# The first inverse transform in pieces of 128 rows by 64 columns, with its first product made between the pieces

## The reference, cut to what matters

```python
x_ft = jnp.fft.rfft2(xt, s=(M, N)) / scale_fwd
a = x_ft[:, :, :nm, :nm]
blk1, blk2 = _complex_matmul_2d(a, fw1), _complex_matmul_2d(a, fw2)
out_ft = out_ft.at[:, :, :nm, :nm].set(blk1)
out_ft = out_ft.at[:, :, N - nm:, :nm].set(blk2)
out = jnp.fft.irfft2(out_ft, s=(N, M)) / scale_bwd
res = out @ W + b
return jax.nn.relu(res + out)
```

## Time and profile before

| what | us |
|---|---|
| median of 3 runs (lowest, highest) | 14682.73 (14680.42, 14685.68) |
| the profiled execution, its own time | 14687.5 |
| its span in the profile | 14685.3 |
| TensorE busy | 10796.8 |
| VectorE busy | 8873.9 |
| ScalarE busy | 6706.6 |
| GpSimd busy | 5138.0 |

### The profile page before, as it was taken

One profiled execution on the slowest core, in us unless ns is written; L12 is line 12 of the kernel. 1 busy time (PEld: TensorE's weight loads), 2 busy tenths in 40 slices (PEclk: granted clock), 3 DMA queues, 4 the chain that ended last, 5 costly groups with the idle time before them and its releaser, 6 DMA issues. The chain is left out here.

```text
span 14685.3 us, 297339 instructions
## 1 busy us (share of the span) xinstructions
PE 10796.8 (74%) x113226; PEld 7857.0 (54%) x113226; DVE 8873.9 (60%) x20267; ACT 6706.6 (46%) x10775; POOL 5138.0 (35%) x3844
## 2 busy tenths in 40 slices
PE   8655665999999999787787879986774677454432
PEld 3243222777777777666666668852322333344432
DVE  3213444777777777788888843322544545599992
ACT  5311222777777777566666632245233444222220
POOL 0002443656555655433333345520000689200001
PEclk9878887999999999999999989998787888555555
DMA  6686775111111111111111159997899666300008
GB/s 261 186 183 187 241 234 188 40 40 43 40 43 40 43 40 41 47 46 70 47 54 62 47 209 363 363 327 257 315 377 384 234 200 221 86 25 23 18 10 324
DMA packets 1298491, 2188.40 MB, mean 149 GB/s; under 512 B 116749, under 2 KB 951069, under 8 KB 1231781
## 3 DMA queue, kind: packets, MB, share of 16 engines
q1 hardware_dynamic: 878084, 1649.47, 33.9%
q10 hardware_dynamic: 398624, 463.54, 8.9%
q0 software_dynamic: 20608, 58.22, 1.4%
HBM read 1371.45 MB, written 799.58 MB: 148 GB/s over the span
## 5 line engine op out<-in xcount | busy, mean ns | idle before, releaser
L781 POOL TENSOR_TENSOR la_s<-la_s,la_mx 128x512 f32<-128x512 f32 x2048 | 2093.2, 1043 | 1458.0 <-DVE la_mx L740 1457.6
L820 ACT ACTIVATE la_et<-la_pt 128x512 f32<-128x512 f32 x2048 | 1120.2, 598 | 723.4 <-PE la_pt L652 723.4
L652 PE MATMUL la_pt<-la_idn,la_s 128*128 128x128 f32 x8192 | 1174.4, 289 | 214.8 <-POOL la_s L781 214.3
L740 DVE TENSOR_REDUCE la_mx<-la_s 128x16 f32<-128x1024 f32 x1024 | 1243.0, 1214 | 17.7
L732 DVE TENSOR_TENSOR la_s<-la_ps,la_post 128x2048 f32<-128x2048 f32 x512 | 1167.5, 2280 | 25.1 <-PE la_ps L638 25.1
L652 PEld LDWEIGHTS la_pt<-la_idn,la_s 128*128 128x128 f32 x8192 | 921.6, 146 | 328.1 <-issue 224.2
L2252 ACT ACTIVATE cs_sm<-cs_sm,cs_gq,cs_tt 8x1 f32<-8x1 f32 x1024 | 395.0, 386 | 1187.6 <-DVE cs_sm L2336 1187.6
L2135 PE MATMUL cs_tb<-cs_tt,cs_sel 8*128 8x16 f32 x2048 | 448.2, 370 | 652.6 <-DVE cs_tt L2334 652.6
L1439 PE MATMUL pj_pp<-pj_pw,pj_at 128*128 128x256 f32 x4096 | 927.5, 380 | 0.0
L956 PE MATMUL gm_xp<-gm_fws,gm_y 128*128 128x258 f32 x2048 | 561.6, 421 | 421.7 <-ACT gm_ri L1040 421.7
L1439 PEld LDWEIGHTS pj_pp<-pj_pw,pj_at 128*128 128x128 f32 x4096 | 759.3, 190 | 92.9
(11 more groups left out here) (327 smaller groups left out, 27151.3 us busy)
## 6 DMA issues: line engine op xcount, KB each, us to landing
f_xt<-in_x SPq DMA_DIRECT2D x128, 1024.0 KB, 7.9
i_xr<-in_x SPq DMA_DIRECT2D x64, 2048.0 KB, 9.0
x<-pj_o SPq DMA_DIRECT2D x64, 2048.0 KB, 10.2
f_xt<-x SPq DMA_DIRECT2D x128, 1024.0 KB, 13.7
i_xr<-x SPq DMA_DIRECT2D x64, 2048.0 KB, 14.5
x<-i_xo ACTq DMA_DIRECT2D x64, 2048.0 KB, 14.6
sp_xt<-x SPq DMA_DIRECT2D x144, 512.0 KB, 4.6
out<-sp_xt SPq DMA_DIRECT2D x144, 512.0 KB, 2.9
```

The costliest lines, as they stand in the source:

```text
L652: last = nc.tensor.transpose(t_bank(S, i)[:, h, :], s[:, S % RS, i, h, :], idn[:, :])
L740: nc.vector.reduce_max(mx[:, S % RS, ts, :].rearrange("p t h -> p (t h)"), s[:, S % RS, ts].rearrange("p t h (d i) -> p (t h d) i", d=2), ...
L781: nc.gpsimd.tensor_tensor(sv, sv, mb, ALU.subtract).then_inc(s_sub, 1)
L820: nc.scalar.activation(et[:, k % RT].rearrange("p h n -> p (h n)"), t_bank(S, i)[:, :, :].rearrange("p h n -> p (h n)"), ACT.Exp).then_inc ...
```

## The change

Each image is cut in 8 pieces again, but of 128 rows and 64 columns (r = k % 2, columns 64 * (k // 2) on), so a piece has the same 2 MB. A load is now 128 runs of 16 KB. A store run is 8 windows of 32 channels, 1 KB, and a piece has two stores of 1 MB; SP asks for them, behind the load of the piece two later. The first product is cut in units of eight channels and 128 columns, 16 units an image (NU = 8 for each half of the columns), eight matmuls each. A unit fills `zp`, two PSUM banks of its own, and waits until the unit before it is emptied. The eight units of the right half are made during pieces 0 to 2 of the image, after the matmuls 1, 3 and 5 of a piece; those of the left half of the next image during pieces 5 to 7. VectorE empties the even ones, behind the additions of one more matmul, ScalarE the odd ones. The squares of a piece are summed in the piece that follows, after its matmul 6. The totals of an image come after piece 0 of the next, the statistics after pieces 1 and 2. The modes of the next image are asked for behind the load of piece 4 and the stores of piece 2. All loops are written out.

```diff
-    WC = 32
-    NP = W // WC
+    WC = 64
+    NP = 2 * W // WC
...
+    ALL = B * NP
+    SPOTS = (1, 3, 5)
...
+        zp = m.ps("zp", [P, 2, 512])
...
+        def unit_at(q, i):
+            b, k = q // NP, q % NP
+            if i not in SPOTS or k in (3, 4):
+                return None
+            n = (k if k < 3 else k - 5) * len(SPOTS) + SPOTS.index(i)
+            if n >= NU or (k > 4 and b + 1 == B):
+                return None
+            return b * 2 * NU + (NU if k < 3 else 2 * NU) + n
...
+                def load(q):
+                    b, k = q // NP, q % NP
+                    r, w0 = k % 2, k // 2 * WC
+                    if q >= 2:
+                        sp.wait_ge(s_fused, (q - 1) * NB)
+                    sp.dma_start(xr[:, q % 2, :], res[b, r * P:(r + 1) * P, w0:w0 + WC, :].rearrange("p w c -> p (w c)"))\
+                        .then_inc(s_x[q % 2], 16)
+                def store(q):
...
+                    sp.wait_ge(s_fused, (q + 1) * NB)
+                    for s, out in enumerate((out_l, out_g)):
+                        sp.dma_start(out[b, r * P:(r + 1) * P, :, n0:n0 + NW, :].rearrange("p u n c -> p u (n c)"),
+                                     xo[:, q % 2, s * CH:(s + 1) * CH].rearrange("p (u m) -> p u m", u=WIN)).then_inc(s_store[q % 2], 16)
+                for q in range(ALL):
+                    load(q)
+                    if q >= 2:
+                        store(q - 2)
+                    if q % NP == 4 and q // NP + 1 < B:
+                        sp.wait_ge(s_u, (q // NP + 1) * 2 * NU)
+                        modes(q // NP + 1)
...
+                def unit(u):
+                    pe.wait_ge(s_zb, 2 * (u // (2 * NU)) + 2)
+                    if u:
+                        pe.wait_ge(s_v[(u - 1) % 2], (u - 1) // 2 + 1)
+                    n = u % NU
+                    for k in range(4):
+                        for h in range(2):
+                            rows = slice(h * kr, (h + 1) * kr)
+                            last = nc.tensor.matmul(zp[:, h, k * P:(k + 1) * P], zv[rows, :, 8 * n + 2 * k + h],
+                                                    km[rows, columns(u)], start=True, stop=True)
+                    last.then_inc(s_u, 1)
...
+                for q in range(ALL):
...
+                    for i in range(NB):
+                        n = q * NB + i
+                        if n >= 4:
+                            pe.wait_ge(s_fused, n - 3)
+                        nc.tensor.matmul(fp[:, n % 4, :], kxm[:, r * P:(r + 1) * P],
+                                         v[:, w0 + i * WIN:w0 + (i + 1) * WIN, :].rearrange("p w c -> p (w c)"),
+                                         start=True, stop=True).then_inc(s_f, 1)
+                        u = unit_at(q, i)
+                        if u is not None:
+                            unit(u)
+                        if i == 6 and q:
+                            if k == 1 and b:
+                                group_sums(b - 1)
+                            squares(q - 1)
...
+                for q in range(ALL):
+                    b, k, j = q // NP, q % NP, q % 2
+                    dve.wait_ge(s_x[j], 16 * (q // 2 + 1))
+                    if q >= 2:
+                        dve.wait_ge(s_store[j], 32 * (q // 2))
+                        dve.wait_ge(s_acc, q - 1)
+                        dve.wait_ge(s_sq, q - 1)
+                    for i in range(NB):
+                        dve.wait_ge(s_f, q * NB + i + 1)
...
+                        last.then_inc(s_fused, 1)
+                        u = unit_at(q, i - 1)
+                        if u is not None and u % 2 == 0:
+                            turn(u)
+                    if k == 0 and b:
+                        totals(b - 1)
...
-                        for s, out in enumerate((out_l, out_g)):
-                            for r in range(2):
-                                act.dma_start(out[bass.ds(b, 1), r * P:(r + 1) * P, :, wc * NW:(wc + 1) * NW, :]
...
+                    act.wait_ge(s_fused, (q + 1) * NB)
+                    if q:
+                        act.wait_ge(s_sum, q)
+                    nc.scalar.activation(sq[:, :], xo[:, q % 2, :], ACT.Square).then_inc(s_sq, 1)
```

More of the change, by code:

```diff
@@ L2552, in _ @@
+                for q in range(ALL):
[5 more added lines that the diff above has]
+                        modes(q // NP + 1)
+                for q in range(ALL - 2, ALL):
+                    store(q)
+                for j in range(2):
+                    sp.wait_ge(s_store[j], 32 * (ALL // 2))
             @block.tensor
@@ L2619, in _ @@
+                squares(ALL - 1)
+                group_sums(B - 1)
             @block.vector
             def _(dve):
[L2621 to L2624 removed]
                 nc.vector.memset(ones[:, :], 1.0).then_inc(s_ones, 1)
@@ L2630, in _, with add_bias, turn, totals @@
                     row = brow[h * kr:h * kr + 1, :]
-                    last = nc.vector.tensor_scalar(row, row, bias_scale, None, ALU.mult)
-                last.then_inc(s_ones, 1)
-                dve.wait_ge(s_ones, 4)
+                    nc.vector.tensor_scalar(row, row, bias_scale, None, ALU.mult).then_inc(s_ones, 1)
+                dve.wait_ge(s_ones, 5)
+                def add_bias(b):
+                    dve.wait_ge(s_z, b * 32 + 32)
+                    for h in range(2):
+                        row = zx[h * kr:h * kr + 1, 0, 0, :]
+                        nc.vector.tensor_tensor(row, row, brow[h * kr:h * kr + 1, :], ALU.add).then_inc(s_zb, 1)
+                def turn(u):
+                    dve.wait_ge(s_u, u + 1)
+                    nc.vector.tensor_copy(*evict(u)).then_inc(s_v[0], 1)
+                def totals(b):
+                    dve.wait_ge(s_acc, b * NP + NP)
+                    if b:
+                        dve.wait_ge(s_tp, b)
+                    for h in range(2):
+                        cs = slice(h * HALF, (h + 1) * HALF)
+                        last = nc.vector.reduce_sum(tot[:, 0, cs], acc[:, h * CH:(h + 1) * CH].rearrange("p (n c) -> p c n", c=HALF),
+                                                    axis=AX.X)
+                    last.then_inc(s_accfree, 1)
+                    dve.wait_ge(s_sum, b * NP + NP)
+                    for h in range(2):
+                        rows, cs = slice(h * 64, (h + 1) * 64), slice(h * HALF, (h + 1) * HALF)
+                        last = nc.vector.reduce_sum(tot[rows, 1, cs], sums[rows, :].rearrange("p (n c) -> p c n", c=HALF), axis=AX.X)
+                    last.then_inc(s_tot, 1)
                 def finish(b):
@@ L2705, in _ @@
+                totals(B - 1)
+                finish(B - 1)
+                deviation(B - 1)
             @block.gpsimd
             def _(pool):
[L2707 to L2717 removed]
+                for q in range(ALL):
+                    b, k = q // NP, q % NP
+                    pool.wait_ge(s_fused, (q + 1) * NB)
+                    if k == 0:
+                        if b:
+                            pool.wait_ge(s_accfree, b)
+                        nc.gpsimd.tensor_copy(acc[:, :], xo[:, q % 2, :]).then_inc(s_acc, 1)
+                    else:
+                        pool.wait_ge(s_acc, q)
+                        nc.gpsimd.tensor_tensor(acc[:, :], acc[:, :], xo[:, q % 2, :], ALU.add).then_inc(s_acc, 1)
@@ L2752, in _ @@
-                for_images(act, body, finish)
-                for j in range(2):
-                    act.wait_ge(s_store[j], (B * (NP // 2) + 1) * 64)
-                act.wait_ge(s_sst, B * 16 + 16)
+                for u in range(1, NU, 2):
+                    turn(u)
+                for q in range(ALL):
+                    b, k = q // NP, q % NP
+                    for i in SPOTS:
+                        u = unit_at(q, i)
+                        if u is not None and u % 2:
+                            turn(u)
+                    if k == 2 and b:
+                        deviation(b - 1)
+                    if k == 3 and b:
+                        put_stats(b - 1)
+                    act.wait_ge(s_fused, (q + 1) * NB)
+                    if q:
+                        act.wait_ge(s_sum, q)
+                    nc.scalar.activation(sq[:, :], xo[:, q % 2, :], ACT.Square).then_inc(s_sq, 1)
```

227 lines of the change are left out of this document (64 added, 163 removed).

## The result

The changed kernel takes 14635.8 us (median of 7 runs, 14629.3 to 14643.7) against 14682.7: a ratio of 0.9967, with a 95% interval of 0.9956 to 0.9977. That is 47 us less (0.33%), where 249 were forecast, and above the range's end of 14600. The profiled execution took 14633.8, with a span of 14632.1.

The account below looks back on a forecast made before the run. Pieces were taken as DMA-bound, the first product as TensorE and evicting engines with DMA idle. Prologue 47.7, images 993 and ending 22.7 gave stage 1063, 249 less, so 14434; 8-in-10 range 14350 to 14600.

Parts of the forecast that it names:

- the working of an image, 128: One image in the stage: pieces 105, totals 7, modes 11, clock 5, against 161 before.
- I take 1.1: First product: one unit of 16 instructions lasts 1.1 us, range 0.9 to 1.5, upper end 2.2 if nothing ran side by side.
- TensorE's whole work for an image: 90: TensorE at full clock: second product, squares and 16 units total 90 us an image, under 12.1 a piece.
- VectorE: ... 72 and a few small ones: VectorE per image: additions, eight evictions and totals total 72 us; small operations not priced.
- my rivals: TensorE cold half the time (0.15, 14592); transfers no cheaper (0.14, 14530); better (0.06, 14290 to 14330); slower (0.05, 14865).
- So 1.5 of wait in each piece that has units: Single `zp`: TensorE waits 1.5 us per piece with units while VectorE empties an even unit behind its addition.
- I take 13: Loading an image's modes, 4.2 MB in the same queue, takes 13 us, between 11.5 and 15.1.
- 1 KB stores at 46.6 ns: Store transfers: 2048 runs of 1 KB at 46.6 ns cost 5.96 us a piece, against 7.05 with 512 bytes.
- That all stores move to SP's queue costs me nothing: Issuing all stores from SP adds no time; ScalarE's freed squares are already counted in the 12.1 a piece.
- The idle third: First product between images, 40.6 us with DMA engines 1% busy, which the change was to fill.
- The clock: TensorE's granted clock above 0.9 after dense work; 5 us an image added for 90 of work.
- DMA share below 0.75 and VectorE waits mostly for `fp`: Sign in the changed stage that the forecast was wrong on the waits.

Follow-up runs that it names:

- with the waits removed: Changed kernel with statistics in PSUM, VectorE emptying units before additions, modes laid out by halves in one 128-partition DMA, two buffers, asked earlier: 14375.1, ratio 0.9791.
- The order alone: Changed kernel with VectorE emptying an even unit before its next addition instead of behind it: 14579.6, ratio 0.9928.
- The transfers alone: Kernel before with 128-row by 64-column pieces, 16 KB loads, 1 KB stores still asked for by ScalarE, first product between images: 14648.4, ratio 0.9974.
- taking its freedom back: Changed kernel with stores asked for by ScalarE again, ahead of the square; loads and modes stay on SP: 14746.5, ratio 1.0043.
- three were joined: Changed kernel with statistics and bias scratch in PSUM, VectorE emptying units before additions, mode load in eight alternating DMAs: 14497.2, ratio 0.9874.

## Why the prediction was wrong

The forecast had the place and the direction right and missed four fifths of the size. What failed is the working of an image, 128, in three of its terms: a unit at 1.1, the small VectorE operations at nothing, and the mode load at 13. By piece, against its own working (13.8 with three units, 12.7 with two, 12.1 without, 7 for totals, 11 for modes, and 5 an image for the clock):

| pieces of the image | forecast | measured | what made the difference |
|---|---|---|---|
| 0 and 6 | 27.6 | 33.4 | six units, 0.92 more each |
| 7 | 12.7 | 16.1 | two units, and a second product partly at a lower granted clock (0.89 in the window) |
| 1, with the totals | 20.8 | 20.4 | none |
| 2 and 3, with the statistics | 24.8 | 41.0 | VectorE held by GpSimd |
| 4 | 12.1 | 8.9 | the load had long landed |
| 5, with the modes | 24.8 | 34.1 | the modes, and the load and stores behind them |
| clock | 5 | | in the rows above |
| sum | 128 | 153.9 | |

26 more an image, by 7.5, are 195 of the 200 that the stage missed.

- **"I take 1.1" for a unit: wrong.** It measured 2.02, near the upper end of 2.2. The Trainium skill's rule beside it ("TensorE: Matmul & The Clock Gate", LDWEIGHTS, estimate 1.7) was nearer. My range took units up to 1.5 only, though I had written 2.2 as the bound. Worth 57 by the run with half of the loads. "TensorE's whole work for an image: 90" fell with it: TensorE was busy 116.4 of the 153.9, and with the waits removed still 89% of 119.7, some 107.
- **"VectorE: ... 72 and a few small ones": wrong by an omission, and a dear one.** I took the small operations at what they last in a kernel in which they run while GpSimd was idle, between images. The change moved them beside GpSimd's additions. Two of them were held 15 an image; 75 in the stage. None of my rivals had it. (GpSimd's 68 are 66 by its rows, 7 x 8.9 + 3.6, which changes nothing.)
- **"So 1.5 of wait in each piece that has units": about right by itself.** 24 of the 49 waits of the stage are 1.21 each, as in the row at 1516.58, 29 in all. But 104 of the 141.5 are fourteen waits of 5.7 to 8.3, two an image: in piece 2, where VectorE's `turn` stands behind the held operation, and in piece 5, where it stands behind the late additions. They follow from the other two losses. The order alone was worth 49, some of it waits that the forecast had priced.
- **"I take 13" for the modes: wrong.** I read 15.1 and 11.5 from stretches where the load ran beside other transfers. Moving the modes alone took 20, at 209 GB/s, in DMAs of 64 partitions; another 12 of the 33 to landing went by behind what was asked for before. With 128 partitions the stage lost 78. The sign was in the kernel before: eight pieces of 13.2 are 106, not the 120.4 of my sum. VectorE's wait of 36.0, where the modes load, fills the gap (the two pieces ahead of it took only some 7 each).
- **1 KB stores at 46.6 ns: right to the digit, and worth nothing here.** A piece with units is 16 to 17 long by TensorE where nothing else holds it, so the DMA engines, at 77%, were no bound. The transfers alone gained 35, but not by this price: their pieces took 13.9. The Trainium skill's rule for 512 bytes ("DMA: Bandwidth & Descriptors", Specifications) misses this price; in the changed kernel, where the run length made no difference, its result would have been the nearer one.
- **"That all stores move to SP's queue costs me nothing": the sign was right, the gain was missed.** I put ScalarE's freedom "inside the 12.1". In the kernel before it was held 32.5 an image, and taking its freedom back costs 117. The one queue has its price in piece 5, where the load and the stores stand behind the modes.
- **The idle third: filled, as forecast.** On the kernel before the transfers alone gave 35 of the 50. The units and the move of the stores to SP, which no run parts, add net some 15, because the losses above took back the rest.
- **The clock: half right.** Squares stayed at 1.92 (125.9 for 64, where 64 x 1.92 = 123), and pieces 4 and 6 had 1.00. Over the image it was 0.87, not above 0.9, with 0.70 in the piece that waits for modes: most likely a consequence of the waits, since with these removed it was 0.93.

The single recoveries, 75 + 57 + 49 and 21 to 78, add up to 202 to 259, which is enough for the missing 200; they overlap somewhat (132 of 145 when three were joined), and part of the 49 was in the forecast. With the losses removed and the bytes of the modes halved, an image took 119.7, less than the forecast 128, with units still at 2.03. My signs for being wrong were half useful: "DMA share below 0.75 and VectorE waits mostly for `fp`" came nearly true (0.76, 401.0 of 490.6) and points at waits, but not at which.

Open: units in which two channels share a load, or a second pair of banks for `zp`, weren't tried (all eight banks are in use); nor was a mode load whose two halves start together in two queues. The stores asked for by SP in the kernel before were not tried either, so how much of its pause the move alone would end is open. Why the pieces with the transfers alone take 13.9 was not settled; that its bias add, 64.3 busy where it was 2.9, took part of its gain is argued only.

## What to carry to other kernels

When work is moved to stand beside another engine's, its small operations have to be priced again: an operation that took 0.2 alone was held for the whole 8.9 of a GpSimd addition, and putting the operands in PSUM gave back 75, more than the 50 that the whole change had brought. A price for matmuls with fresh weights is to be counted in loads and taken from a row with the same number of row groups, and the cover of a load must be set against its time to landing, which hung here on how many partitions one DMA spans and on what stands ahead of it in its queue. Before the change, account for every stretch of the time: a steady rate that does not add up to the whole (8 x 13.2 against 120.4) hides a pause. After filling an idle stretch, read who is waiting in each piece of it before tuning the transfers: here 512-byte and 1 KB stores made no difference, and the order of two instructions made 49.

## What the runs showed of the hardware that I had not expected

- A `tensor_scalar` on [128, 64] in SBUF takes 0.2 alone and 8.77 beside a GpSimd addition of 8.87; with its operands in PSUM 0.23. A `tensor_tensor` of one row with two SBUF inputs was long too (8.88 in one case of the kernel with the transfers alone, from 0.21); with one input in PSUM its mean was 0.21 again.
- Loads of 64 partitions ran at 209 GB/s with the 16 DMA engines shown as 96% busy, one of 128 partitions at 431. Alternating the halves in one queue came to 225.
- Sixteen weight loads of a unit in two row groups set its length: 2.02, against 1.25 for eight loads and the same columns.
- Asking for half a kilobyte held ScalarE for 22.5 while 4.2 MB of modes were on their way in SP's queue, and asking for two stores held it for 32.5 in the kernel before. What in the DMA engines holds it, no run shows.
